# Cross-attention block: the order of the first row maxima, and batch 1 prepared before the first scores

## The chip, the cores and the metric

One core of one Trainium2 chip. The metric is the device time of one execution in microseconds (us), the median of three runs.

## The reference, cut to what matters

```python
B, S, D, H = 4, 512, 256, 16          # DK = 16 features per head; the context has 1024 keys
x = x + xattn(layernorm(x), ctx, ctx, mask)
x = x + ffn_block(layernorm(x))        # 4-token attention, then top-2 of 8 experts

def xattn(q, k, v, mask):
    query, key_, value = rope(heads(q @ w_q.T)), rope(heads(k @ w_k.T)), heads(v @ w_v.T)
    scores = einsum('bhqd,bhkd->bhqk', query, key_) / sqrt(DK)
    scores = where(mask == 0, -10000.0, scores)
    return merge(softmax(scores) @ value) @ w_o.T
```

The change lies in the cross-attention alone; the second block follows it and is the same in both kernels.

## The kernel before

**What is computed per batch.** For each of four batches `b` the kernel normalizes and turns the queries' input (jobs `xn`, `xT`), projects queries, keys and values (`q`, `k`, `v`; `c` is the split of a half of the context, 512 keys, into a high and a low float32r part), rotates queries and keys (`rope`, part 2 for queries, parts 0 and 1 for the two halves of the keys) and stores the rotated pieces to `q_pieces` and `k_pieces` in HBM. From there they are loaded again, regrouped by head, into `qst` and `kst`, three buffers each, one for every unit of eight heads.

**Maxima, then scores.** The softmax subtracts a row maximum that is found beforehand. A quad is four heads of one batch; there are 16. For each quad, 16 jobs `max` (two pairs of heads `hp`, four tiles of queries `qt`, two halves of the keys `kh`) each make two score products on TensorE into one of two buffers `wide`, and VectorE reduces each buffer (L749). Then `nm` and `mxt` turn the maxima into rows, ScalarE copies them to `mxp` (L603), and two DMAs put them into `qst` (L382). Only then can the quad's scores be made: 8 groups to a quad, 128 groups in all. A group is four scores (L942), four exponentials on ScalarE (L609) and, one group later, four products with the values (L957).

**Who does what, in which order.** Each engine runs its instructions in a written order. `attention_order` gives it: the list `before` is the opening, up to the first scores, and the list `timed` puts each job at a time counted in groups. All engines follow that one order, each for the jobs that it has a part in. A projection comes in pieces: the projections of `before` are mostly whole (512 columns), those in `timed` halves of 256 columns, six matmuls each. In the opening, batch 0 is prepared whole, and the keys of batch 1 (`k`, 1, 0 before the maxima of quad 0, `k`, 1, 1 after them). `xn` and `xT` of batch 1 stand in groups 0 and 2, its queries in groups 4 to 7, its values in groups 13 to 20. `xn` is four VectorE instructions (L701) from SBUF to SBUF.

**The queue of SP.** Stores and loads stand in one order of their own on SP, each with its waits, so an issue waits for all those ahead of it. In the opening it is:

```python
        store_turned(0, 2)                 # queries of batch 0
        store_turned(0, 1)                 # keys of batch 0, half 1
        load_keep(1, 0)
        load_queries(0, slice(0, 2))
        load_keys(0, slice(0, 2), (1,))
        load_queries(0, slice(2, PAIRS))
        store_turned(0, 0)
        load_keys(0, slice(0, 2), (0,))
        load_keys(0, slice(2, PAIRS))
        load_context(1, 1)
```

then unit 1, `load_keep(1, 1)`, `load_max_rows(0)` and the stores of batch 1's keys. The rotation of batch 1 and later is GpSimd's (L449 to L463), which also splits these context halves (L497, L466).

Of the kernel before, what the change touches and what calls it, by code (L numbers as in the profile page):

```python
# [36 lines left out]
LEAD = 3  # L37


def final(order, *begin):  # L40

    return next(j for j in reversed(order) if j[:len(begin)] == begin)


def attention_order():


    def maxes(quad):
        return [("max", quad, hp, qt, kh) for hp in range(2) for qt in range(QT) for kh in range(2)] + [("nm", quad), ("mxt", quad)]
# [4 lines left out]
    before += [("rate", 1), ("c", 1, 0), ("k", 1, 0, 0), ("k", 1, 0, 1), ("rope", 1, 0), ("c", 1, 1)] + maxes(0)  # L54
    before += [*maxes(1)[:2], ("k", 1, 1, 0), *maxes(1)[2:AHEAD], ("k", 1, 1, 1), ("rope", 1, 1)]

    timed = []
    for b in range(B):
        g, t = 32 * b, b + 1
        if t < B:  # L60
            timed += [(max(g - 3.5, 0), ("xn", t)), (g + (0.5 if b else 2.5), ("xT", t))]
            timed += [(g + x, ("q", t, n // 2, n % 2)) for n, x in enumerate((3, 4, 6, 7) if b else (4, 5, 6, 7))] + [(g + 7.5, ("rope", t, 2))]
            timed += [(g + 13.2 + n, ("v", t, n // 4, n // 2 % 2, n % 2)) for n in range(8)]
        if t + 1 < B:
            timed += [(g + 16.5, ("c", t + 1, 0)), (g + 20.5, ("c", t + 1, 1))]
            timed += [(g + 21.2 + n, ("k", t + 1, n // 4, n // 2 % 2, n % 2)) for n in range(8)] + [(g + 24.5, ("rope", t + 1, 0)), (g + 28.5, ("rope", t + 1, 1))]
        if b > 0:
            timed += [(g + 2.2, ("oT", b - 1))] + [(g + x, ("oP", b - 1, n // 2, n % 2)) for n, x in enumerate((8, 10, 11, 12))]
# [38 lines left out]
def cross_attention(nc, ctx, io, xt, wide, narrow, values, ident, mv1, rates, split_dram, list_dram):  # L107
# [3 lines left out]
    def sb(name, shape, dt=F32):  # L111
        return ctx.enter_context(nc.sbuf_tensor(name, shape, dt))
# [14 lines left out]
    rstd = sb("rstd", [P, NT])  # L127
    xT_hi = sb("xT_hi", [P, KC, SQ], F32R)
# [24 lines left out]
    aT_lo = sb("aT_lo", [P, KC, SQ], F32R)  # L153
    mask_i, mask_s = attn[0:B * KT, 0, 0:P].bitcast(I32), attn[0:B * KT, 1, 0:P]
# [8 lines left out]
    c_in, first_in, quad_in = sem("c_in"), sem("first_in"), sem("quad_in")  # L163
# [8 lines left out]
    var_set, std_set = sem("var_set"), sem("std_set")  # L172
# [12 lines left out]
    def on_act(j):  # L185
        return j[0] in ("w", "xT", "v", "mxt", "oT", "oT0", "oT1", "root0") or (j[0] in ("q", "k") and not turned_by_dve(j))
# [4 lines left out]
    def on_dve(j):  # L191
        return j[0] in ("xn", "xT", "max", "nm", "out", "oT", "oT0", "oT1", "oP", "oP1", "moments", "tile0", "again0", "rates0") or j in (("c", 0, 0), ("c", 0, 1)) or j in BY_DVE or (j[0] in ("q", "k") and turned_by_dve(j)) or (j[0] == "w" and not lo_by_pool(j))
# [108 lines left out]
    c_blocks = [(j[1], j[2]) for j in order if j[0] == "c" and j[1:] != (0, 0)]  # L301
# [9 lines left out]
    def _(sp):  # L311
# [32 lines left out]
        def landed(u, heads):  # L344
            return quad_in if u == 0 and heads.start == 0 else stack_in[u % 3]
# [123 lines left out]
    def _(pool):  # L469
# [20 lines left out]
        for j in order:  # L490
            if not on_pool(j):
                continue
            if j[0] == "c":
                b, g = j[1:]
                pool.wait_ge(c_in, 16 * (c_blocks.index((b, g)) + 1))
                pool.wait_ge(*by_pe(last_of("v", b - 1, g)))
                step(nc.gpsimd.tensor_copy(c_hi[g][:, :, :], craw[:, :, :]))  # L497
                settle()
                lower(nc.gpsimd, c_lo[j[2]], craw, c_hi[j[2]]).then_inc(pool_done, 1)
# [44 lines left out]
    def _(act):  # L544
# [15 lines left out]
        def job(j):  # L560
# [89 lines left out]
    def _(dve):  # L650
# [6 lines left out]
        def settle():  # L657

            dve.wait_ge(dve_step, steps[0])

        def statistics(i, batches):
# [13 lines left out]
            settle()  # L675

# [6 lines left out]
        for j in order:  # L683
# [12 lines left out]
            if kind == "xn":  # L696
                b = j[1]
                if b > 0:
                    dve.wait_ge(*by_pe(("xT", b - 1)))
                for t in range(QT):  # L700
                    last = nc.vector.tensor_scalar(xn[:, t, :], xt[:, QT * b + t, :], mv[:, QT * b + t, 0:1],  # L701
                                                   rstd[:, QT * b + t:QT * b + t + 1], ALU.subtract, ALU.mult)
# [107 lines left out]
    def _(pe):  # L810
# [60 lines left out]
        def job(j):  # L871
# [14 lines left out]
            if kind == "xT":  # L886
                pe.wait_ge(*by_dve(("xn", j[1])))
# [1028 lines left out]
```

## Time and profile before

| | us |
|---|---|
| median of 3 runs | 795.62 (795.46 to 797.01) |
| the profiled execution | 792.0 |
| its span in the trace | 790.2 |
| first matmul of the maxima | 61.14 |
| first matmul of the scores | 88.68 |
| copy of `outT` of the last quad | 509.7 |

TensorE is busy for 698.4 us (88%), VectorE 562.5 (71%), ScalarE 488.0 (62%), GpSimd 355.1 (45%). Times in the trace count from the span's start. `L621` is the copy of `outT` that ScalarE makes at the end of each quad, so the differences between its starts time eight groups each. "PEclk" is the clock that TensorE was granted: 1.00 is 2.4 GHz and 0.50 is 1.2 GHz.

### The profile page before, as it was taken

The numbers are of one execution on the slowest core, as the hardware profiler recorded it, in microseconds if no ns is written. First come the engines' busy times: TensorE is split into PE (matmuls) and PEld (weight loads), VectorE is DVE, ScalarE is ACT, GpSimd is POOL, SyncE is SP. The second block draws the span as 40 slices with busy tenths as digits, with TensorE's granted clock in tenths as the row PEclk, the third lists the DMA queues.
The fourth block names the chain that finished last, engine by engine and source line by source line (L and its number), as shares of the span: only waits on it lengthen the run. The fifth ranks groups of instructions, "written<-read, shape, count | busy, mean of one in ns | idle before, by whom it ended". The sixth has DMA issues, their size and how long they took to land. (4 is left out here: it accounts for less than half of the span.)

```text
span 790.2 us, 13501 instructions
## 1 busy us (share of the span) xinstructions
PE 698.4 (88%) x4402; PEld 428.4 (54%) x4402; DVE 562.5 (71%) x930; ACT 488.0 (62%) x968; POOL 355.1 (45%) x262
## 2 busy tenths in 40 slices
PE   3256689999999998999999999988978889999996
PEld 2252334444344443444433443476767779999995
DVE  4958778778788778788798984367997426555653
ACT  2010348777677776777778777856746047667673
POOL 4966425118604139345938880000045713544444
PEclk9775769999899999999999999999989799999999
DMA  9576246766667664326877870059736546623321
GB/s 256 187 235 183 104 150 190 229 160 204 213 207 243 174 187 160 115 83 197 292 250 244 274 265 6 1 156 409 249 67 179 223 109 143 117 31 40 39 28 20
DMA packets 59719, 130.73 MB, mean 165 GB/s; under 512 B 8868, under 2 KB 26308, under 8 KB 58196
## 3 DMA queue, kind: packets, MB, share of 16 engines
q1 hardware_dynamic: 33364, 72.86, 28.4%
q0 software_dynamic: 16848, 35.95, 17.8%
q10 hardware_dynamic: 9440, 21.06, 9.0%
q8 instruction: 38, 0.62, 0.3%
q14 instruction: 29, 0.24, 0.1%
HBM read 80.80 MB, written 69.39 MB: 190 GB/s over the span
## 5 line engine op out<-in xcount | busy, mean ns | idle before, releaser
L749 DVE TENSOR_REDUCE mx<-wide 128x2 f32<-128x1024 f32 x256 | 307.5, 1223 | 76.4 <-PE wide L903 74.9
L609 ACT ACTIVATE probs<-narrow 128x512 f32<-128x512 f32 x492 | 265.5, 599 | 87.7 <-PE narrow L942 86.6
L903 PE MATMUL wide<-kst,qst 49*128 49x512 f32 x512 | 181.1, 481 | 22.2 <-DVE mx L749 12.6
L942 PE MATMUL narrow<-qst,kst 51*128 51x512 f32 x492 | 188.8, 458 | 1.9 <-ACT probs L609 1.5
L942 PEld LDWEIGHTS narrow<-qst,kst 51*128 51x128 f32 x492 | 80.7, 189 | 135.8 <-issue 57.9
L957 PE MATMUL values<-probs,vaug 128*17 128x512 f32 x1024 | 139.0, 616 | 1.4 <-ACT probs L609 0.8
L1707 POOL DMA_INDIRECT out<-res,token x39 | 60.8, 1558 | 91.4 <-DMA out<-res,token 60.3
L903 PEld LDWEIGHTS wide<-kst,qst 49*128 49x128 f32 x512 | 74.7, 199 | 36.6 <-DVE mx L749 23.1
L454 POOL TENSOR_TENSOR turn_b<-turn_a,tab 128x1024 f32<-128x1024 f32 x10 | 24.1, 2410 | 69.8 <-ACT turn_a L603 69.2
L1239 POOL DMA_DIRECT2D out<-xt x4 | 5.5, 1376 | 108.5 <-DVE xt L1434 108.5
L1732 ACT ACTIVATE h_hi<-narrow 128x512 fp32r<-128x512 f32 x39 | 23.3, 598 | 41.3 <-PE narrow L1812 41.3
L1758 DVE TENSOR_TENSOR h_lo<-narrow,h_hi 128x512 fp32r<-128x512 f32 x39 | 27.0, 692 | 23.4 <-ACT h_hi L1732 23.4
L957 PEld LDWEIGHTS values<-probs,vaug 128*17 128x17 f32 x1024 | 17.1, 96 | 44.7 <-issue 30.0
L1246 POOL DMA_INDIRECT list_rows<-lists,rows_to x32 | 32.3, 1008 | 17.2 <-issue 8.5
L1754 DVE TENSOR_TENSOR y_lo<-y_full,y_hi 128x256 fp32r<-128x256 f32 x39 | 16.6, 426 | 28.9 <-ACT y_hi L1719 28.9
L449 POOL TENSOR_SCALAR keep<-keep 128x512 f32<-128x512 int32 x7 | 13.7, 1962 | 50.3 <-ACT turn_a L603 50.3
L1719 ACT ACTIVATE y_hi<-wide,lncol 128x128 fp32r<-128x128 f32 x78 | 36.3, 465 | 0.0
L1718 ACT ACTIVATE y_full<-wide,lncol 128x128 f32<-128x128 f32 x78 | 35.8, 459 | 0.1
L497 POOL CAST c_hi<-craw 128x1024 fp32r<-128x1024 f32 x6 | 6.2, 1037 | 60.7 <-PE narrow L817 57.9
L603 ACT ACTIVATE mxp<-narrow 8x512 f32<-8x512 f32 x16 | 9.2, 574 | 33.2 <-PE narrow L908 33.2
L603 ACT ACTIVATE vaug<-narrow 128x256 f32<-128x256 f32 (+1 forms) x28 | 11.7, 418 | 28.5 <-PE narrow L817 27.4
L817 PE MATMUL narrow<-wv_hi,c_hi 128*128 128x256 f32 x64 | 16.5, 343 | 14.3 <-POOL wv_lo L466 14.3
(287 smaller groups left out, 1370.1 us busy)
## 6 DMA issues: line engine op xcount, KB each, us to landing
list_rows<-in_w ACTq DMA_DIRECT2D x56, 342.0 KB, 4.7
kst<-k_pieces SPq DMA_DIRECT2D x14, 784.0 KB
k_pieces<-turn_a SPq DMA_DIRECT2D x16, 512.0 KB, 4.6
w_hi<-w_hi SPq DMA_DIRECT2D x16, 512.0 KB, 10.8
w_lo<-w_lo SPq DMA_DIRECT2D x16, 512.0 KB, 11.6
turn_a<-in_w POOLq DMA_DIRECT2D x11, 512.0 KB, 5.6
w_hi<-turn_b POOLq DMA_DIRECT2D x11, 512.0 KB, 3.0
w_lo<-turn_a POOLq DMA_DIRECT2D x11, 512.0 KB, 4.7
```

Source lines behind the costliest of these rows:

```text
L454: step(engine.tensor_tensor(z[:, :, :], a[:, :, :], cos, ALU.mult))
L609: nc.scalar.activation(probs[:, n % NP, :], score_bank(n), ACT.Exp, scale=DK ** -0.5).then_inc(exp_done, 1)
L749: last = nc.vector.tensor_reduce(mx[quad % 2][:, qt, :, hp, kh], slot[:, :, :], axis=AX.X, op=ALU.max)
L903: last = nc.tensor.matmul(slot[:, i, :], qst[u % 3][r:r + R_MAX, h, P * qt:P * qt + P], kst[u % 3][r:r + R_MAX, h, 512 * kh:512 * kh + 512 ...
L942: nc.tensor.matmul(score_bank(n), kst[u % 3][r:r + R_ALL, h, P * kt:P * kt + P], qst[u % 3][r:r + R_ALL, h, :], start=True, stop=True).the ...
L957: last = nc.tensor.matmul(values[32 * hq:32 * hq + DK + 1, :], vaug[b % 2][:, kt, h, :], probs[:, (4 * g + hq) % NP, :], start=kt == 0, st ...
L1246: pool.indirect_dma_start(list_dram, bass.IndirectOffsetOnAxis(rows_to[:, j, i, s:s + 1], 0), lists[j][:, i, s, :].bitcast(U32), None).the ...
L1707: pool.indirect_dma_start(out, bass.IndirectOffsetOnAxis(token[:, n:n + 1], 0), res[n % PIECES][:, :], None, bounds_check=TOKENS - 1, oob_ ...
L1718: nc.scalar.activation(yT[n % 2][:, k, :], y_banks[n % 2][:, k, :], ACT.Identity, **affine)
L1719: last = nc.scalar.activation(yT_hi[n % 2][:, k, :], y_banks[n % 2][:, k, :], ACT.Identity, **affine)
L1732: nc.scalar.activation(hT_hi[n % 2][:, :, :], h_banks[n % 2], ACT.Copy).then_inc(h_hi_set, 1)
L1758: nc.vector.tensor_tensor(hT_lo[n % 2][:, :, :], h_banks[n % 2], hT_hi[n % 2][:, :, :].bitcast(F32), ALU.subtract).then_inc(h_lo_set, 1)
```

## The change

1. The 16 maxima of quad 0 are made in another order: the eight on keys of half 1 first, then the eight on half 0. The first waits for the queries and half 1 alone (`quad_in`, 64); the ninth waits for half 0 (`half_in`, 32). SP issues the store and the load of half 0 ahead of the queries of pairs 2 and 3.
2. The second half of batch 1's context gets a buffer of its own (`next_raw`, which is `xn`'s memory), loaded at about 20 us, and leaves its place after unit 0's loads.
3. Batch 1's keys come as eight half pieces, one after each of the first eight maxima; its values, formerly in groups 13 to 20, as eight half pieces after the maxima 9 to 12, after `nm` and after the first two maxima of quad 1. `xT` of batch 1 stands after the eighth maximum.
4. `xn` of batches 1 to 3 goes to ScalarE, as one activation per tile with scale `rstd` and bias `shift` (one new small VectorE instruction), for batches 2 and 3 one tile to a group.
5. `PLAN` gives the places of all jobs of batches 2 and 3 in the groups, and SP's order in the loop is changed to fit. For batch 2: `c` in groups 3 and 12 (before 16 and 20), keys in 9 to 19 (before 21 to 28), `xn` in 18 to 21 (before 28), `xT` in 24 (before 32), queries in 26 to 30 (before 35 to 39), values in 36 to 44 (before 45 to 52). Batch 1's queries stand in groups 2 to 5.

```diff
+PLAN = [(18, (26, 27, 28, 30), (), (3, 12), (9, 10, 11, 14, 16, 17, 18, 19), ()),
+        (None, (), (4, 5, 6, 7, 9, 10, 11, 12), (7, 16), (18, 19, 20, 22, 23, 24, 25, 27), (13, 14, 15, 16)),
+        (-6, (3, 4, 6, 7), (13, 14, 15, 16, 17, 18, 19, 20), (), (), (8, 10, 11, 12)),
+        (None, (), (), (), (), (8, 10, 11, 12))]
...
-    before += [("rate", 1), ("c", 1, 0), ("k", 1, 0, 0), ("k", 1, 0, 1), ("rope", 1, 0), ("c", 1, 1)] + maxes(0)
-    before += [*maxes(1)[:2], ("k", 1, 1, 0), *maxes(1)[2:AHEAD], ("k", 1, 1, 1), ("rope", 1, 1)]
+    before += [("rate", 1), ("c", 1, 0), ("c", 1, 1)] + [("xn", 1, n) for n in range(QT)]
+    keys, vals = [[(kind, 1, n // 4, n // 2 % 2, n % 2) for n in range(8)] for kind in "kv"]
+    first = [("max", 0, hp, qt, kh) for kh in (1, 0) for hp in range(2) for qt in range(QT)]
+    for n, j in enumerate(first):
+        before += [j] + (keys + vals)[n:n + 1] * (n < 12) + [("rope", 1, 0)] * (n == 3) + [("rope", 1, 1)] * (n == 7) + [("xT", 1)] * (n == 7)
+    before += [("nm", 0), vals[4], vals[5], ("mxt", 0)] + maxes(1)[:2] + vals[6:] + maxes(1)[2:AHEAD]
...
+        sp.wait_ge(*by_pe(("xT", 0)))
+        sp.dma_start(next_raw, io["ctxT"][:, SK + 512:2 * SK].rearrange("(k p) t -> p k t", p=P)).then_inc(next_in, 16)
...
         load_keys(0, slice(0, 2), (1,))
-        load_queries(0, slice(2, PAIRS))
         store_turned(0, 0)
         load_keys(0, slice(0, 2), (0,))
+        load_queries(0, slice(2, PAIRS))
         load_keys(0, slice(2, PAIRS))
-        load_context(1, 1)
...
+            if t + 1 < B:
+                load_context(t + 1, 1)
             load_max_rows(4 * b + 2)
             if t < B:
                 load_queries(2 * t)
+            load_max_rows(4 * b + 3)
             if t + 1 < B:
-                load_context(t + 1, 1)
-            load_max_rows(4 * b + 3)
+                store_turned(t + 1, 0)
             if t < B:
                 load_queries(2 * t + 1)
                 load_keys(2 * t + 1)
                 load_max_rows(4 * b + 4)
             if t + 1 < B:
-                store_turned(t + 1, 0)
                 store_turned(t + 1, 1)
...
+            if kind == "xn":
+                b, t = j[1:]
+                if t == 0:
+                    act.wait_ge(*by_pe(("xT", b - 1)))
+                    if b == 1:
+                        act.wait_ge(*by_pool(("c", 1, 1)))
+                    act.wait_ge(shift_set, 1)
+                n = QT * b + t
+                nc.scalar.activation(xn[:, t, :], xt[:, n, :], ACT.Identity, scale=rstd[:, n:n + 1], bias=shift[:, n:n + 1]).then_inc(act_done, 1)
...
-                if (quad, hp, qt, kh) == (0, 0, 0, 0):
-                    pe.wait_ge(quad_in, 96)
+                if (quad, hp, qt) == (0, 0, 0):
+                    pe.wait_ge(*((quad_in, 64) if kh == 1 else (half_in, 32)))
```

## Rows read from the trace of the kernel before

**Rows 1.** Page, the span in 40 slices: granted TensorE clock in tenths.

```profile
PEclk9775769999899999999999999999989799999999
```

**Rows 2.** Windows; columns: PE, PEld, DVE, ACT, POOL busy, PEclk, DMA share, GB/s.

```profile
140.00:180.00 40.00, 40.00 (x272) 18.87 (x272) 31.04 (x33) 31.63 (x64) 6.86 (x4) 1.00 0.70 200
```

**Rows 3.** Timeline 40 to 62 us: start, duration, engine, line, operands, idle before.

```profile
43.96 0.66 SPq L371 DMA_DIRECT2D kst<-k_pieces  x2
...
45.73 1.04 POOL L497 CAST c_hi<-craw 128x1024 fp32r<-128x1024 f32 x1 [3.53 <-PE narrow L817]
45.76 0.42 SPq L339 DMA_DIRECT2D k_pieces<-turn_a  x1
...
46.85 2.39 POOL L466 TENSOR_TENSOR c_lo<-craw,c_hi 128x1024 fp32r<-128x1024 f32 x1
...
50.69 0.23 DVE L674 RECIPROCAL rstd<-std 128x12 f32<-128x12 f32 x1 [0.28 <-ACT std L565]
...
55.87 1.41 SPq L371 DMA_DIRECT2D kst<-k_pieces  x4
...
61.14 1.22 PE L903 MATMUL wide<-kst,qst 49*128 49x512 f32 x4 [8.76 <-DMA kst<-k_pieces]
```

**Rows 4.** Timeline 62 to 92 us: quad 0's maxima and the first scores.

```profile
62.05 18.19 DVE L749 TENSOR_REDUCE mx<-wide 128x2 f32<-128x1024 f32 x16 [11.13 <-PE wide L903]
...
82.07 0.59 ACT L603 ACTIVATE mxp<-narrow 8x512 f32<-8x512 f32 x1 [29.06 <-PE narrow L908]
82.69 1.45 SPq L382 DMA_DIRECT2D qst<-mxp  x2
...
88.68 0.50 PE L942 MATMUL narrow<-qst,kst 51*128 51x512 f32 x1
...
90.81 1.55 ACT L609 ACTIVATE probs<-narrow 128x512 f32<-128x512 f32 x3
```

**Rows 5.** Source L328, the load of `keep` issued at 59.5 us: landing.

```profile
DMA to landing us min/median/max: 23.8/23.8/23.8
```

**Rows 6.** Windows, while unit 1's keys are loaded.

```profile
74.00:78.00 4.00, 2.69 (x8) 0.86 (x6) 4.00 (x5) 0.00 (x0) 0.66 (x1) 0.50 0.44 180
```

**Rows 7.** Timeline 89 to 112 us: `xn`, `xT` of batch 1, a rotation on GpSimd.

```profile
89.47 1.94 POOL L449 TENSOR_SCALAR keep<-keep 128x512 f32<-128x512 int32 x1 [14.81 <-ACT turn_a L603]
...
91.50 2.40 POOL L451 TENSOR_TENSOR turn_a<-turn_a,keep 128x1024 f32<-128x1024 f32 x1
...
93.36 6.89 DVE L701 TENSOR_SCALAR xn<-xt,mv,rstd 128x256 f32<-128x256 f32 x4
...
102.55 2.35 POOL L463 TENSOR_TENSOR turn_b<-turn_b,turn_a 128x1024 fp32r<-128x1024 f32 x1
...
106.96 1.97 PE L890 MATMUL wide<-ident,xn 128*128 128x128 f32 x8 [0.89 <-DVE mx L749]
...
108.96 1.02 ACT L603 ACTIVATE xT_hi<-wide 128x1024 fp32r<-128x1024 f32 x1 [2.62 <-PE wide L890]
...
109.30 0.45 SPq L321 DMA_DIRECT2D craw<-in_ctxT  x1
...
110.09 1.22 DVE L727 TENSOR_TENSOR xT_lo<-wide,xT_hi 128x1024 fp32r<-128x1024 f32 x1 [2.05 <-PE wide L903]
```

**Rows 8.** Windows in the two stalls after `xn`.

```profile
96.00:98.00 2.00, 0.00 (x0) 0.00 (x0) 2.00 (x2) 0.00 (x0) 1.92 (x2) 0.81 0.00 0
196.00:200.00 4.00, 1.65 (x11) 0.75 (x8) 3.93 (x9) 1.73 (x4) 3.92 (x3) 0.95 0.19 73
```

**Rows 9.** Source L621 in successive windows: count, ns, first and last start.

```profile
L621 ACT ACTIVATE outT<-values x3: 598/600/606, 127.6 to 178.8; 128x512 f32<-128x512 f32 x3
...
L621 ACT ACTIVATE outT<-values x4: 597/598/599, 209.4 to 290.4; 128x512 f32<-128x512 f32 x4
...
L621 ACT ACTIVATE outT<-values x1: 599/599/599, 237.1 to 237.1; 128x512 f32<-128x512 f32 x1
...
L621 ACT ACTIVATE outT<-values x4: 597/597/599, 320.6 to 399.8; 128x512 f32<-128x512 f32 x4
...
L621 ACT ACTIVATE outT<-values x1: 597/597/597, 374.5 to 374.5; 128x512 f32<-128x512 f32 x1
...
L621 ACT ACTIVATE outT<-values x1: 600/600/600, 422.0 to 422.0; 128x512 f32<-128x512 f32 x1
```

**Rows 10.** DMA view, issues: KB each, median us to landing.

```profile
craw<-in_ctxT SPq DMA_DIRECT2D x7, 512.0 KB, 6.6
```

**Rows 11.** Groups on ScalarE after 600 us: count, busy and mean ns.

```profile
L1719 ACT ACTIVATE y_hi<-wide,lncol 128x128 fp32r<-128x128 f32 x78 | 36.3, 465 | 0.0
...
L1734 ACT ACT_TABLE_LOAD x1 | 1.3, 1283 | 19.3 <-PEq L1882 19.3
```

More of the change, by code:

```diff
@@ L59, in attention_order @@
         g, t = 32 * b, b + 1
[L60 to L66, printed above, removed]
+        x, q, v, c, k, o = PLAN[b]
+        if b == 0:
+            timed += [(n + 2.2, ("q", 1, n // 2, n % 2)) for n in range(4)] + [(5.5, ("rope", 1, 2))]
+        if x is not None:
+            r = 2 if b == 0 else t
+            timed += [(g + x + n, ("xn", r, n)) for n in range(QT)] + [(g + x + 6.2, ("xT", r))]
+            timed += [(g + at + 0.2, ("q", r, n // 2, n % 2)) for n, at in enumerate(q)] + [(g + q[-1] + 0.5, ("rope", r, 2))]
+        timed += [(g + at + 0.2, ("v", t, n // 4, n // 2 % 2, n % 2)) for n, at in enumerate(v)]
+        if k:
+            timed += [(g + at + 0.5, ("c", t + 1, n)) for n, at in enumerate(c)]
+            timed += [(g + at + 0.2, ("k", t + 1, n // 4, n // 2 % 2, n % 2)) for n, at in enumerate(k)] + [(g + k[4 * n + 3] + 0.5, ("rope", t + 1, n)) for n in range(2)]
         if b > 0:
-            timed += [(g + 2.2, ("oT", b - 1))] + [(g + x, ("oP", b - 1, n // 2, n % 2)) for n, x in enumerate((8, 10, 11, 12))]
+            timed += [(g + 2.2, ("oT", b - 1))] + [(g + at + 0.2, ("oP", b - 1, n // 2, n % 2)) for n, at in enumerate(o)]
     for quad in range(QUADS - 1):
@@ L95, in attention_order @@
     for b in range(1, B):
-        assert index[("xT", b - 1)] < index[("xn", b)] and index[final(order, "q", b - 1)] < index[("xT", b)]
+        assert index[("xT", b - 1)] < index[("xn", b, 0)] and index[final(order, "q", b - 1)] < index[("xT", b)]
         assert all(index[final(order, "v", b - 1, g)] < index[("c", b, g)] for g in range(2))
@@ L127, in cross_attention @@
     rstd = sb("rstd", [P, NT])
+    shift = sb("shift", [P, NT])
     xT_hi = sb("xT_hi", [P, KC, SQ], F32R)
@@ L185, in on_act @@
     def on_act(j):
-        return j[0] in ("w", "xT", "v", "mxt", "oT", "oT0", "oT1", "root0") or (j[0] in ("q", "k") and not turned_by_dve(j))
+        return j[0] in ("w", "xT", "v", "mxt", "oT", "oT0", "oT1", "root0") or j[0] == "xn" and j[1] > 0 or (j[0] in ("q", "k") and not turned_by_dve(j))
     def lo_by_pool(j):
@@ L191, in on_dve @@
     def on_dve(j):
-        return j[0] in ("xn", "xT", "max", "nm", "out", "oT", "oT0", "oT1", "oP", "oP1", "moments", "tile0", "again0", "rates0") or j in (("c", 0, 0), ("c", 0, 1)) or j in BY_DVE or (j[0] in ("q", "k") and turned_by_dve(j)) or (j[0] == "w" and not lo_by_pool(j))
+        return j[0] in ("xT", "max", "nm", "out", "oT", "oT0", "oT1", "oP", "oP1", "moments", "tile0", "again0", "rates0") or j in (("xn", 0),) or j in (("c", 0, 0), ("c", 0, 1)) or j in BY_DVE or (j[0] in ("q", "k") and turned_by_dve(j)) or (j[0] == "w" and not lo_by_pool(j))
     def on_pool(j):
@@ L299, in set_before @@
         return in_sets[in_sets.index(j) - 2] if j in in_sets[2:] else None
-    c_blocks = [(j[1], j[2]) for j in order if j[0] == "c" and j[1:] != (0, 0)]
+    c_blocks = [(j[1], j[2]) for j in order if j[0] == "c" and j[1:] not in ((0, 0), (1, 1))]
     k_blocks = [j for j in blocks if j[2] < 2]
@@ L342, in stored, with landed @@
             sp.wait_ge(*sets_stored(("rope", b, part)))
-        def landed(u, heads):
-            return quad_in if u == 0 and heads.start == 0 else stack_in[u % 3]
+        def landed(u, heads, parts=(0, 1)):
+            if u == 0 and heads.start == 0:
+                return half_in if parts == (0,) else quad_in
+            return stack_in[u % 3]
         def freed(u):
@@ L494, in _ @@
                 b, g = j[1:]
[L495 removed]
+                if (b, g) == (1, 1):
+                    pool.wait_ge(next_in, 16)
+                else:
+                    pool.wait_ge(c_in, 16 * (c_blocks.index((b, g)) + 1))
+                raw = next_raw if (b, g) == (1, 1) else craw[:, :, :]
                 pool.wait_ge(*by_pe(last_of("v", b - 1, g)))
[L497 removed]
+                step(nc.gpsimd.tensor_copy(c_hi[g][:, :, :], raw))
                 settle()
[L499 removed]
+                nc.gpsimd.tensor_tensor(c_lo[g][:, :, :], raw, c_hi[g][:, :, :].bitcast(F32), ALU.subtract).then_inc(pool_done, 1)
             elif j[0] == "w":
@@ L675, in statistics @@
             settle()
+            if i > 0:
+                nc.vector.scalar_tensor_tensor(out=shift[:, tiles], in0=mv[:, tiles, 0], scalar=-1.0, in1=rstd[:, tiles], op0=ALU.mult, op1=ALU.mult).then_inc(shift_set, 1)
         def masks():
@@ L751, in _ @@
                 quad = j[1]
-                dve.wait_ge(*by_dve(("max", quad, 1, QT - 1, 1)))
+                dve.wait_ge(*by_dve(last_of("max", quad)))
                 step(nc.vector.tensor_reduce(nm[:, :, :, :], mx[quad % 2][:, :, :, :, :], axis=AX.X, op=ALU.max, negate=True))
```

16 lines of the change are left out of this document (7 added, 9 removed).

## The prediction

> **What bounds the kernel now.** I read the page's slices first, then the windows, the timeline of the opening, the waits in it, and at last the ends of the quads. From about 110 us to 500 us TensorE's clock is nearly always full; the digits below it stand at the start, near 200 and near 310 us [rows 1]. In an undisturbed stretch of the groups TensorE is busy all 40 us of 40, VectorE and ScalarE 31 to 32 [rows 2]: there only TensorE's work counts, and work of other engines costs only when TensorE has to wait for it.
>
> Before the groups it is otherwise. The first maxima wait for keys: SP issues the last of their loads at 55.87, after a store that it issued from 45.76, and TensorE starts at 61.14 after 8.8 us idle. The load of half 1 had been issued at 43.96, and VectorE was free from 50.92 [rows 3]. The 16 maxima then take 18.19 us, 1.14 each, set by VectorE. `mxp` is ready at 82.66, its DMAs are issued from 82.69, the first score starts at 88.68 (TensorE has 1.2 GHz and the keys of batch 1 in between) and the first exponential at 90.81, after a table load [rows 4]. Meanwhile SP's queue drains slowly: the load of `keep`, issued at 59.5, lands 23.8 us later, at 83.3 [rows 5], while the DMA engines move only 180 GB/s at a share of 0.44, as if about 7 of the 16 worked [rows 6]. The key loads cover 49 partitions each; what stands behind them on those engines waits.
>
> Inside the groups there are three stalls. `xn` of batch 1 takes 6.89 us on VectorE beside GpSimd's rotation [rows 7]; TensorE is idle throughout 96 to 98 and loses its clock, and the same comes after `xn` of batch 2, with 1.65 us busy of 4 [rows 8]. The quads' ends price them [rows 9]. Groups 88 to 95 hold no projection and take 422.0 - 399.8 = 22.2 us. Groups 80 to 87 hold five half pieces and take 25.3, so a half piece costs 3.1 / 5 = 0.62. Groups 24 to 31, with five pieces and `xn`, take 209.4 - 178.8 = 30.6, where 22.2 + 3.1 = 25.3 would do: 5.3 lost. Groups 56 to 63, alike, take 30.2: 4.9 lost. Groups 32 to 39 with four pieces, `xT` and `oT` take 27.7, so `xT` and `oT` cost 3.0 together. The first eight groups take 127.6 - 88.7 = 38.9.
>
> **The change, part by part. The opening.** The first maximum needs the queries and half 1 alone. Half 0's load was used 61.14 - 55.87 = 5.3 us after its issue, so half 1, issued at 43.96, is there by about 50; VectorE is free at 51.2 (50.92 and `shift`, about as long as `rstd`). First maximum reduced from about 52 instead of 62.05: -10. The second context half costs no time: loaded at 20 us while TensorE's data is in hand, split on GpSimd right after the first (cast 1.04 and difference 2.39, so done near 52.8) [rows 3]; ScalarE's four `xn` follow to about 54.5, under 0.5 each (a copy four times as large took 1.02 [rows 7]). They block the key pieces' copies until then, but three pieces fit the ring, and the fourth comes near 55.5: no stall. Eight maxima with a key piece each: TensorE has 0.62 for the piece and up to 0.5 for the pair, VectorE 1.14; I take 1.2 a step, 9.6, to 61.6. If the clock were 1.2 GHz, a step would cost 1.24 for the piece and 0.8 for the pair (four matmuls took 1.22 [rows 3]), 2.0, which I keep for the upper end. `xT`: transposes 1.97 at half clock, copy 1.02, difference 1.22 [rows 7]; one transposing step overlaps the last maximum, so 2.8 net, to 64.4. Eight more maxima, four with a value piece: 4 x 1.2 + 4 x 1.14 = 9.4, to 73.8. From the last maximum's end (80.24) to `mxp`'s (82.66) it was 2.4 [rows 4]: 76.2. SP then issues the rows until 77.7.
>
> Here stands the choice. If the rows land at once, about 1.5 us after, scores start near 79; the last pieces and four maxima of quad 1 fill TensorE until then. If the rows queue behind unit 1's keys as `keep` did, they wait until the queue drains. That was at 83.3. In the new order half 0's store is issued 0.4 us sooner and without 384 KB of queries in front, and 512 KB of context are gone behind it; at the rates of [rows 6] that is some 2 us: 81.2. I take the queue, since a DMA issued on it did wait 23.8 us [rows 5], and scores from 81.7: **-7.0**. The ends are 79 and 85. The Trainium skill (DMA: Bandwidth & Descriptors, "Why a DMA increments its semaphore by 16 and not by 1") says that a transfer issued from SP is split over the largest number of engines up to 16 that divides the outermost dimension, the lowest-numbered of them: 7 for 49 partitions, 2 for the row pairs. By that rule the rows are on two of the seven loaded engines and queue; without it the sum would be 2.7 lower. The trace agrees so far as the share of 0.44 goes [rows 6].
>
> **Groups 0 to 7.** They lose `xn`, `xT`, the stretch at half clock and the table load, which now falls into the wait for the rows. What stays is 22.2 + 4 x 0.62 = 24.7, and 2.3 for the lag from a first score to a quad's end and two groups with three maxima (3.4 of VectorE against about 2.8): 27.0 for 38.9, **-11.9**.
>
> **Groups 8 to 63** took 320.6 - 127.6 = 193.0 [rows 9]. In `PLAN` they hold 32 pieces (4, 4, 4, 4, 7, 6, 3 by quad) where there were 40: 7 x 22.2 + 32 x 0.62 + 3.0 = 178.2. (The same for before: 183.2, and 10 of stalls is what [rows 9] showed.) Eight of `xn` now cut into ScalarE's exponentials, 0.4 each; ScalarE has 8.4 of 40 us free [rows 2], 0.6 a group, so most of it fits, and I add 1.5 for what delays an exponential.
>
> Then the moved jobs' due times. `keep` for rotation (1, 1) lands near 81.2 now as well. A rotation takes 89.47 to 104.90 = 15.4; its store, two `keep` loads and the context's issue took from 104.9 to 109.3 = 4.4 [rows 7]; the context lands 6.6 after that [rows 10] and its split is 3.5: 111.1, against the key pieces due at the end of group 9, near 112. Batch 1's query rotation behind it on GpSimd takes 15.4 less its first two instructions (4.3) = 11.1, to 122.2. Behind its store on SP now stand context (2, 1) and the maxima's rows of quad 2, which land at 122.2 + 2.4 for the issues + 6.6 = 131.2, and the split at 134.7; due are the rows at group 16, near 131, and the pieces at its end, near 134. So two items are just in time or late by a microsecond or two: +2. Together 178.2 + 1.5 + 2 = 181.7: **-11.3**. From group 64 on the order is the same, and the second block too: 0. Its weights are split by GpSimd after the last rotation, in the same group as before.
>
> **Sum.** -7.0 - 11.9 - 11.3 = -30.2. Against the profiled execution's 792.0 that is 761.8; the median is 3.6 above the profiled one, so 765.4, said as 765.
>
> **Rivals.** *Slow clock and late chain.* TensorE had 1.2 GHz while it made maxima alone [rows 6], and it may keep it in the opening, since VectorE paces it again. Twelve steps at 2.0 instead of 1.2 are +9.6, from 76.2 to 85.8 for `mxp`, scores near 89.5: +7.8; or group 16 waits 5 us and loses 3 more of clock. 773 to 781. For it: [rows 1, 8]. Against: a piece's 0.62 doubles TensorE's work in those steps.
>
> *Rows not held up.* The rows land at once: 762.5, inside my range.
>
> *Chain decides (slower).* In SP's queue, store of batch 1's queries, context and rows of quad 2 hang on GpSimd, which hangs on `keep`. Every microsecond past group 16's start is TensorE's, and once it passes the 30 saved elsewhere, near 163 us for the rows, the kernel is slower: two rotations more than I count, and 800 or above. Nothing in the rows asks for two.
>
> *The function table.* If `Identity` had to reload ScalarE's table between exponentials, each `xn` would cost two loads of 1.28: eight are 20.5, and 4.9 more in the opening hidden, so 786, and near no change with the clock lost too. Against: 78 activations of that kind stand beside the gelu with one load before them all [rows 11].
>
> *The early start gives nothing.* The rows queue to 85: opening -3.7 instead of -7.0: 769.
>
> **Chances.** Forecast with its near cases (rows at 79 to 85): 0.70, alone 758 to 772. Slow clock or late chain: 0.18. Table: 0.04. Chain decides, or something like it: 0.04. No effect for another reason: 0.02. Better than the sum (stalls cost more than counted): 0.02. The range 755 to 781 takes in the first two. What a measurement can tell from no change is 0.2%, 1.6 us. Faster 0.93, same 0.02, slower 0.05.
>
> **What would show it.** First `max` matmul near 51 to 52; first score at 80 to 83, its wait ended by the DMA of `mxp`; end of quad 0 near 109; 24 to 26 us for each of the quads 1 to 3, no window of idle TensorE near 200 or 310. Wrong would be: half 1 landing after 55; clock 0.50 through the maxima; a wait at group 9 or 16 for a split or for rows of over 3 us; table loads among the exponentials.

## The result: 1.1% faster, and outside the range

| | before | changed |
|---|---|---|
| median, same chip (us) | 796.2 (795.46 to 797.01, 4 runs) | 787.93 (783.22 to 791.12, 4 runs) |
| profiled execution, its span | 792.0, 790.2 | 785.13, 783.3 |
| first score | 88.68 | 86.14 |
| end of quad 0, end of quad 15 | 127.6, 509.7 | 115.6, 499.3 |

The ratio is 0.9886, with a 95% interval of 0.9838 to 0.9934: 8 us of gain where 30 were forecast, and a time above the upper end of the range.

The ends of the quads again are the starts of the copy of `outT`, now L653, in successive windows; they answer to [rows 9].

```profile
L653 ACT ACTIVATE outT<-values x3: 598/598/598, 115.6 to 166.3; 128x512 f32<-128x512 f32 x3
...
L653 ACT ACTIVATE outT<-values x1: 599/599/599, 270.5 to 270.5; 128x512 f32<-128x512 f32 x1
...
L653 ACT ACTIVATE outT<-values x1: 597/597/597, 306.3 to 306.3; 128x512 f32<-128x512 f32 x1
...
L653 ACT ACTIVATE outT<-values x2: 598/598/599, 336.0 to 362.2; 128x512 f32<-128x512 f32 x2
...
L653 ACT ACTIVATE outT<-values x6: 597/598/653, 387.8 to 499.3; 128x512 f32<-128x512 f32 x6
```

Six quads, groups 8 to 55, take 270.5 - 115.6 = 154.9. Then groups 56 to 63 take 306.3 - 270.5 = 35.8 where they took 30.2, and the next eight 29.7. The windows show both places: the old stall near 200 us is gone, a new one stands at 293 to 303 us, and with it comes the slow clock. They answer to [rows 8].

```profile
196.00:200.00 4.00, 4.00 (x27) 2.08 (x28) 3.60 (x5) 2.85 (x6) 3.07 (x2) 1.00 0.89 290
292.00:296.00 4.00, 1.64 (x12) 0.36 (x12) 2.61 (x3) 1.94 (x4) 3.77 (x5) 1.00 0.47 178
296.00:300.00 4.00, 0.00 (x0) 0.00 (x0) 0.00 (x0) 0.00 (x0) 2.21 (x1) 0.50 0.55 210
300.00:304.00 4.00, 0.78 (x4) 0.50 (x4) 0.00 (x0) 0.00 (x0) 0.00 (x0) 0.50 0.95 344
```

What TensorE waits for there is in the waits of 272 to 306 us (us in total, times, longest):

```profile
PE narrow L972 <- DMA qst<-mxp: 9.6, 1, 9.6
```

Those are the maxima's rows of quad 8. SP's queue in the timeline of that stretch shows what was issued just ahead of them:

```profile
281.58 0.38 SPq L353 DMA_DIRECT2D k_pieces<-turn_a  x1
...
283.37 2.76 SPq L374 DMA_DIRECT2D qst<-q_pieces  x2
286.24 0.95 SPq L387 DMA_DIRECT2D kst<-k_pieces  x2
288.82 1.29 SPq L398 DMA_DIRECT2D qst<-mxp  x2
```

In the kernel before, the same rows had 27 us between the loads of unit 5 and themselves, and the stores came behind them (its timeline, 280 to 316 us):

```profile
283.55 0.80 SPq L358 DMA_DIRECT2D qst<-q_pieces  x2
284.46 0.61 SPq L371 DMA_DIRECT2D kst<-k_pieces  x2
311.44 1.28 SPq L382 DMA_DIRECT2D qst<-mxp  x2
312.76 0.40 SPq L339 DMA_DIRECT2D k_pieces<-turn_a  x1
```

The change put the store of batch 3's first keys, ready at 281, ahead of unit 5's loads, so these were issued just ahead of the rows; 8 KB then landed at 303.2, 14.4 us after their issue. While TensorE stood still the DMA engines moved 178 to 210 GB/s at a share of 0.47 to 0.55, the picture of [rows 6].

The opening, in the timeline from 48 us, which answers to [rows 3, 4]:

```profile
48.64 0.50 PE L933 MATMUL wide<-kst,qst 49*128 49x512 f32 x2 [1.74 <-DMA kst<-k_pieces]
...
49.08 2.04 DVE L704 TENSOR_SCALAR varc<-mv 128x12 f32<-128x12 f32 x1
...
51.75 3.48 DVE L779 TENSOR_REDUCE mx<-wide 128x2 f32<-128x1024 f32 x3
...
58.46 1.23 DVE L779 TENSOR_REDUCE mx<-wide 128x2 f32<-128x1024 f32 x1 [1.07 <-PE wide L933]
...
79.39 2.36 POOL L469 TENSOR_TENSOR turn_a<-turn_a,keep 128x1024 f32<-128x1024 f32 x1
79.67 0.19 DVE L783 TENSOR_REDUCE nm<-mx 128x16 f32<-128x32 f32 x1
79.89 1.88 DVE L787 CAST mh<-nm 128x16 fp32r<-128x16 f32 x1
...
83.38 1.45 SPq L398 DMA_DIRECT2D qst<-mxp  x2
...
85.45 1.28 ACT L658 ACT_TABLE_LOAD   x1
...
86.14 0.50 PE L972 MATMUL narrow<-qst,kst 51*128 51x512 f32 x1
```

The first maximum starts even sooner than forecast. Then VectorE, which should pace these steps, waits 1.07 us in each for TensorE: a step takes 2.3 us, with the clock at 0.50 from 50.2 to 67.3 us. The page shows the clock over the whole span, beside [rows 1]; the dip near 300 us is the stall above.

```profile
PEclk9767799999999995999999999999998889999999
```

### The profile page after: what moved, and what is told of

Read it like the earlier page. It is cut to its first block and busy times, and to the rows that moved or that the text cites. A ratio compares the mean times of both kernels' runs of the same rounds, so it can differ in the third digit from the quotient of the medians.

```text
span 783.3 us, 13563 instructions
## 1 busy us (share of the span) xinstructions
PE 701.2 (90%) x4426; PEld 433.2 (55%) x4426; DVE 559.5 (71%) x919; ACT 494.7 (63%) x984; POOL 354.7 (45%) x262
## 3 DMA queue, kind: packets, MB, share of 16 engines
q1 hardware_dynamic: 33364, 72.86, 27.7%
## 5 line engine op out<-in xcount | busy, mean ns | idle before, releaser
L933 PE MATMUL wide<-kst,qst 49*128 49x512 f32 x512 | 174.3, 467 | 7.3 <-DVE mx L779 3.9
L972 PEld LDWEIGHTS narrow<-qst,kst 51*128 51x128 f32 x492 | 80.1, 188 | 144.3 <-ACT probs L641 53.5
L987 PE MATMUL values<-probs,vaug 128*17 128x512 f32 x1024 | 137.3, 608 | 1.4 <-ACT probs L641 0.8
L933 PEld LDWEIGHTS wide<-kst,qst 49*128 49x128 f32 x512 | 71.7, 191 | 19.4 <-DVE mx L779 12.5
L472 POOL TENSOR_TENSOR turn_b<-turn_a,tab 128x1024 f32<-128x1024 f32 x10 | 24.1, 2412 | 58.6 <-ACT turn_a L635 58.1
L1748 ACT ACTIVATE y_full<-wide,lncol 128x128 f32<-128x128 f32 x78 | 35.8, 460 | 2.2 <-PE wide L1819 2.2
L847 PE MATMUL narrow<-wv_hi,c_hi 128*128 128x256 f32 x64 | 16.6, 345 | 14.4 <-POOL wv_lo L484 14.4
L1833 PE MATMUL wide<-w_hi,y_hi 128*128 x78 | 28.6, 448 | 0.0
```

Source lines behind the costliest of these rows:

```text
L933: last = nc.tensor.matmul(slot[:, i, :], qst[u % 3][r:r + R_MAX, h, P * qt:P * qt + P], kst[u % 3][r:r + R_MAX, h, 512 * kh:512 * kh + 512 ...
L972: nc.tensor.matmul(score_bank(n), kst[u % 3][r:r + R_ALL, h, P * kt:P * kt + P], qst[u % 3][r:r + R_ALL, h, :], start=True, stop=True).the ...
L987: last = nc.tensor.matmul(values[32 * hq:32 * hq + DK + 1, :], vaug[b % 2][:, kt, h, :], probs[:, (4 * g + hq) % NP, :], start=kt == 0, st ...
L1748: nc.scalar.activation(yT[n % 2][:, k, :], y_banks[n % 2][:, k, :], ACT.Identity, **affine)
L1833: last = nc.tensor.matmul(up_banks[n % 2], a[n % 2][:, k, :], w[:, bass.ds(e, 1), k, :].rearrange("p e n -> p (e n)"), start=(i, k) == (0, ...
```

## The experiments

The first four kernels ran beside the kernel before on one chip, the next four on a second, the last three on a third. On the second and third, what follows the end of quad 15 takes 293 to 296 us and not 283 to 285, so medians are compared as ratios to the kernel before on the same chip. The expectations give times for the first chip: a ratio of 0.9715 would be 773.5 us there, 0.9633 would be 767.0. In the table `A` is the end of quad 0 and `B` the time from there to the end of quad 15, both in the profiled execution.

| kernel | A | B | ratio, 95% interval |
|---|---|---|---|
| before | 127.6 | 382.1 | 1 |
| changed | 115.6 | 383.7 | 0.9886, 0.9838 to 0.9934 |
| `a_loads_first` | 119.1 | 384.3 | 0.9866, 0.9835 to 0.9898 |
| `b_rows_first` | 118.4 | 382.4 | 0.9842, 0.9783 to 0.9901 |
| `c_xn_scalar` | 117.4 | 376.7 | 0.981, 0.9783 to 0.9837 |
| `d_opening_alone` | 116.6 | 378.4 | 0.9858, 0.983 to 0.9886 |
| `e_loads_first_once` | 117.3 | 370.5 | 0.9715, 0.9669 to 0.9761 |
| `f_rows_by_scalar` | 116.4 | 404.4 | 1.017, 1.0105 to 1.0236 |
| `g_filled_gap` | 110.5 | 371.3 | 0.9633, 0.9591 to 0.9676 |
| `h_keys_ahead` | 114.6 | 371.5 | 0.9733, 0.9666 to 0.98 |
| `i_changed_again` | 112.6 | 387.4 | 0.9847, 0.9796 to 0.9897 |
| `j_old_groups` | 114.5 | 372.3 | 0.9633, 0.9602 to 0.9663 |
| `k_clock_held` | 113.5 | 370.3 | 0.9678, 0.9651 to 0.9706 |

`B` holds a wait that differs between two executions of the same program. Groups 96 to 103 take 23.9 us in the kernel before and 24.3 in the changed one, but 28.3 when the changed one ran again (`i_changed_again`) and 28.4 in `d_opening_alone`. In `i_changed_again` VectorE's cast to `mh` falls beside an instruction of GpSimd there and ends with it:

```profile
421.38 2.36 POOL L556 TENSOR_TENSOR turn_a<-turn_a,turn_b 128x1024 fp32r<-128x1024 f32 x1
...
421.48 2.29 DVE L787 CAST mh<-nm 128x16 fp32r<-128x16 f32 x1
```

TensorE waits 1.5 us for it, and the clock is at 0.50 from 424.9 to 431.7 us. (`a_loads_first` has a cast of 2.27 us at that place but keeps its clock: 26.2.) So the windows of single quads say more than `B` where a difference is under 5 us.

**Unit loads ahead of the store, in every batch** (`a_loads_first`).

```diff
             load_max_rows(4 * b + 3)
-            if t + 1 < B:
-                store_turned(t + 1, 0)
             if t < B:
                 load_queries(2 * t + 1)
                 load_keys(2 * t + 1)
+            if t + 1 < B:
+                store_turned(t + 1, 0)
+            if t < B:
                 load_max_rows(4 * b + 4)
```

> The changed kernel with one move in SP's loop: unit 5's (and 3's) queries and keys are issued before the store of the next batch's keys, not after it. Theory 1: in the changed kernel the maxima's rows of quad 8 land late because they are issued right behind the keys of unit 5, which had waited behind that store; TensorE idles 9.6 us at group 64 and then works at half clock. Then the quad of groups 56 to 63 falls from 35.8 us to 24 to 26, the next from 29.7 to 27 to 28, and the kernel is 11 to 14 us faster than the changed one: 774 to 777. Rival: the late rows are caused by ScalarE's normalizations in groups 58 to 61 delaying the maxima; then the quad stays above 32 us and the time above 783.

The quads' ends put groups 56 to 63 at 25.2 us, so that stall was the order of SP's queue. But groups 24 to 31 now take 37.8. Now it is the store of batch 2's keys that stands behind unit 3's, in the timeline of SP's queue, the waits of 176 to 196 us and a window:

```profile
165.44 0.84 SPq L387 DMA_DIRECT2D kst<-k_pieces  x2
166.33 0.57 SPq L353 DMA_DIRECT2D k_pieces<-turn_a  x1
```

```profile
ACT turn_a L636 <- DMA k_pieces<-turn_a: 10.4, 1, 10.4
...
PE narrow L973 <- ACT turn_a L636: 9.2, 1, 9.2
```

```profile
184.00:188.00 4.00, 0.00 (x0) 0.00 (x0) 0.00 (x0) 0.00 (x0) 0.00 (x0) 0.60 0.25 98
```

ScalarE can't free the piece's buffer before the store has landed, its exponentials wait behind it, and TensorE waits for them: whatever stands right behind a unit's key load pays.

**Rows ahead of the unit loads** (`b_rows_first`): `load_max_rows(4 * b + 4)` moved ahead of `load_queries(2 * t + 1)`, the store first.

> The changed kernel, the store left where the change put it, but the rows of quads 4 and 8 issued before the loads of queries and keys of units 3 and 5. Theory 1: only the place behind the keys matters, so the gain is the same as with the loads first, 11 to 14 us against the changed kernel, 774 to 777, unless the keys themselves then come late for quads 6 and 10. Rival (the store itself, 1.5 MB, holds the rows up): gain under 5 us, 783 or more.

Groups 56 to 63 take 25.2 again, but groups 32 to 39 take 32.3. The rows of quad 5 wait behind the unit load and all that has heaped up behind it, in the waits of 212 to 230 us:

```profile
PE narrow L972 <- DMA qst<-mxp: 4.3, 1, 4.3
```

**Unit 5 alone** (`e_loads_first_once`): as `a_loads_first`, but only where `b == 1`.

> The changed kernel with unit 5's loads ahead of the store of batch 3's keys, the first pass of the loop (unit 3) left as the change has it. Theory 1 (whatever SP issues behind a pair of key loads lands late, be it rows or a store): the quads of groups 24 to 31 and 32 to 39 as in the changed kernel (25.7 and 26.3), those of 56 to 63 and 64 to 71 at 25.2 and 27.7 as with both moved; no wait of over 4 us left in the groups; 774 to 777. Rival (a stall merely moves to the next place): 783 or more.

No stall is left: groups 56 to 63 take 25.2 and the next eight 27.7, `B` falls by 13.2 to 370.5. The timeline has the loads at 266 us and 23 us between them and the rows:

```profile
265.96 0.88 SPq L374 DMA_DIRECT2D qst<-q_pieces  x2
266.95 0.61 SPq L387 DMA_DIRECT2D kst<-k_pieces  x2
...
283.21 0.38 SPq L353 DMA_DIRECT2D k_pieces<-turn_a  x1
...
290.46 1.28 SPq L398 DMA_DIRECT2D qst<-mxp  x2
```

**The rows from ScalarE's queue** (`f_rows_by_scalar`). Does the wait lie in SP's order of issue, or behind the bytes?

```diff
             nc.scalar.activation(dst, src, ACT.Copy).then_inc(act_done, 1)
+            if kind == "mxt":
+                rows_by_scalar(act, j[1])
```

> The changed kernel, but the DMAs of the maxima's rows are issued by ScalarE right after the copy to mxp, so they stand in ScalarE's queue; SP's order else as changed. If the rows wait because they stand in one queue behind the keys, the wait at group 64 goes: that quad near 25, 774 to 779, with some 0.5 to 1 us for each quad's two issues on ScalarE. If they wait because the engines are full whatever the queue, the quad stays above 32 us and the time above 783.

The rows still wait: groups 56 to 63 take 34.4 us, above the 32 of the second branch, and the kernel is 1.7% slower than before. In the waits of 290 to 330 us:

```profile
PE narrow L978 <- DMA qst<-mxp: 7.6, 1, 7.6
```

There is a new wait as well. SP no longer waits for a quad's rows before it issues a unit's loads, so unit 3's loads go out at 156.7 to 160.2 us, ahead of the rows of quad 3, and these, on a queue of their own, still land 10.6 us after their issue. In the timeline:

```profile
162.20 1.41 ACTq L583 DMA_DIRECT2D qst<-mxp  x2
...
172.85 0.79 PE L978 MATMUL narrow<-qst,kst 51*128 51x512 f32 x1 [4.69 <-DMA qst<-mxp]
```

So the rows wait behind the bytes of the key load, not behind SP's instructions. The Trainium skill (DMA: Bandwidth & Descriptors, "Why a DMA increments its semaphore by 16 and not by 1") has transfers issued from either queue use the lowest-numbered engines, so that a second queue brings no other engines; this run agrees. `B` is 404.4 us, 20.7 more than in the changed kernel. The new wait and ScalarE's 1.4 us for each quad's two issues are in it; how much each costs is not settled.

**xn on ScalarE alone** (`c_xn_scalar`): the kernel before, with part 4 of the change and nothing else.

```diff
-            timed += [(max(g - 3.5, 0), ("xn", t)), (g + (0.5 if b else 2.5), ("xT", t))]
+            timed += [(g - 3.5 + n if b else 0.5 * n, ("xn", t, n)) for n in range(QT)] + [(g + (0.5 if b else 2.5), ("xT", t))]
```

> The kernel before with one part of the change: the normalization of batches 1 to 3 goes to ScalarE, one tile to a group (batch 1: two in group 0 and two in group 1), all else as before. By my step (stalls of 5.3 and 4.9 us after it in groups 24 to 31 and 56 to 63, and some 6 to 9 in groups 0 to 7 with the lost clock, less 1.5 for ScalarE): 778 to 783, 13 to 18 us faster. Rival (the stalls come from the transposes of xT or the maxima that follow, which stay): 790 or more.

781.1 against 796.9: this part alone gives 15.8 us, twice what the whole change gives. Groups 24 to 31 take 26.6 for 30.6, groups 56 to 63 26.6 for 30.2, and quad 0 ends 10.2 sooner. The window near 200 us holds no idle TensorE:

```profile
196.00:200.00 4.00, 3.98 (x25) 1.75 (x24) 3.06 (x3) 3.43 (x7) 3.85 (x4) 1.00 0.56 172
```

**The opening alone** (`d_opening_alone`): the changed kernel's opening, and the groups, SP's loop and `xn` of batches 2 and 3 as before.

> The changed opening with the order of batches 2 and 3 and SP's loop as before, normalization of batches 2 and 3 on VectorE as before. First score near 86 as in the changed kernel, quad 0 ends near 116, eight value pieces fewer in the groups (-4.6), the stalls at groups 28 and 60 and their clock as before. By the sum of the two traces: 12 at quad 0's end and 4.6 for the pieces, so 778 to 781. Rival (the early start is given back by late loads in quads 1 to 3, which the new order of batch 2 was needed for): 785 or more.

0.9858, 11 us. In the trace `A` falls by 11.0, where the forecast had 18.9 for the opening and groups 0 to 7; the first score starts at 87.8 us, behind 2.3 us steps again. The eight value pieces that leave the groups are worth the 5.0 us forecast: groups 8 to 23 take 46.2 for 51.2. `B` falls by 3.7 alone because groups 96 to 103 take 4.5 more, by the wait told above.

The two `xn` stalls tell something more. `xn` is on VectorE, and TensorE waits 2.3 us for the quad's maxima behind it, as in the kernel before [rows 8], but here the clock stays at 1.00:

```profile
180.00:184.00 4.00, 1.71 (x12) 0.77 (x8) 3.93 (x9) 1.85 (x4) 3.92 (x3) 1.00 0.19 73
```

Groups 24 to 31 take 28.0 us, for 30.6 in the kernel before (whose clock is at 0.50 from 199.6 to 206.5) and 26.6 in `c_xn_scalar`. So of the 4.0 us of that stall about 1.4 are the wait and 2.6 the slow clock behind it, which this kernel's profile doesn't have.

**The clock in the opening** (`g_filled_gap`): `e_loads_first_once`, and 14 small matmuls, whose result nothing uses, ahead of the first maximum.

```diff
+                if j == ("max", 0, 0, 0, 1):
+                    for i in range(14):
+                        nc.tensor.matmul(slot[:, 0, 0:P], ident[:, :], ident[:, :], start=True, stop=True)
```

> As e_loads_first_once, with 14 unused 128-column matmuls on TensorE before the first maximum, where it waits for the keys. Theory 2 (the first eight steps take 2.3 us instead of 1.2 because TensorE is at half clock, and the clock falls for the idle time before the first maximum): clock 1.00 from 48 to 60, steps of 1.2 to 1.4, first score 6 to 8 us sooner, 768 to 771. Rival (the clock falls all the same, since maxima of 49 rows and VectorE's pace leave TensorE too idle): first score within 2 us of the changed kernel's, 774 to 777.

778.36 against 785.48 for `e_loads_first_once` on the same chip: 7.1 us. The filler closes TensorE's idle time ahead of the first maximum; then the clock is 1.00 from 48 to 72 us, and VectorE's eight reductions stand in one row without a wait. In its timeline:

```profile
48.08 3.29 PE L933 MATMUL wide<-ident 128*128 128x128 f32 x28
...
53.11 9.73 DVE L783 TENSOR_REDUCE mx<-wide 128x2 f32<-128x1024 f32 x8
...
75.22 0.17 DVE L791 CAST mh<-nm 128x16 fp32r<-128x16 f32 x1
```

**Four key pieces ahead of the first maximum** (`h_keys_ahead`), real work in the filler's place.

> As e_loads_first_once, but the four key pieces of half 0 of batch 1 stand before the first maximum, where TensorE waits anyway, those of half 1 between maxima 1 to 4, the values after the next eight. Theory 2: eight pieces at half clock in the way of the maxima become four, and dense work before them may hold the clock: first score 3 to 8 us sooner, 768 to 774. Rival (the place of the pieces is not what costs): within 2 us of e_loads_first_once.

784.96, no better than `e_loads_first_once`: the gap is filled, but four pieces delay the first maximum to 53.5 us, and the clock is slow at 75 to 99 us instead.

**The changed kernel again, on a third chip** (`i_changed_again`).

> The changed kernel itself, beside the other two on one chip, so that its own differences to them can be read without a change of chip. All theories: 0.985 to 0.99 of the kernel before; quad 7 (groups 56 to 63) 35 to 36 us and the next 29 to 30, since the rows of quad 8 stand behind unit 5's loads; clock at 0.50 from 50 to 67 us in the maxima with key pieces.

`B` has the stall (302.9 to 331.8 is 28.9 us for groups 64 to 71, the eight before them 35.9). The opening is the surprise. This execution of the very same program kept its clock:

```profile
52.60 9.71 DVE L779 TENSOR_REDUCE mx<-wide 128x2 f32<-128x1024 f32 x8
...
76.87 1.45 SPq L398 DMA_DIRECT2D qst<-mxp  x2
...
82.17 0.50 PE L972 MATMUL narrow<-qst,kst 51*128 51x512 f32 x1 [2.32 <-DMA qst<-mxp]
```

The window of 56 to 60 us is at 1.00 here,

```profile
56.00:60.00 4.00, 4.00 (x27) 2.87 (x26) 3.82 (x5) 1.15 (x3) 2.80 (x2) 1.00 0.82 209
```

and at 0.50 in the changed kernel's first profile, where TensorE gets 18 matmuls done instead of 27:

```profile
56.00:60.00 4.00, 4.00 (x18) 3.07 (x16) 2.45 (x2) 0.38 (x1) 1.80 (x1) 0.50 0.96 213
```

In both, TensorE was idle about 1.7 us for the keys just before the maxima. So the clock behind that gap differs from execution to execution. Of the six profiled executions in which TensorE was idle there for 1.3 to 2.2 us, five fell to 0.50 within 2 us of the first maximum, and this one did not. `f_rows_by_scalar`, idle for 0.4 us, kept 1.00, and so did the four kernels with the gap filled.

The spread of the times isn't this clock alone: it is 8 and 11 us for the changed kernel, 3.9 for `e_loads_first_once`, 2.8 for `g_filled_gap`, and the execution shown here took 796.95, 8 us above the fastest of its six, though its opening kept the clock.

**Before's groups, with the opening and xn** (`j_old_groups`): `g_filled_gap`'s opening, `xn` on ScalarE, but batches 2 and 3 in the groups of the kernel before and SP's old loop.

> The changed kernel's opening with the gap ahead of the first maximum filled by 14 small matmuls (they write nothing that is used), but batches 2 and 3 in the groups in which they stand in the kernel before, with SP's old order in the loop, and their xn on ScalarE, one tile to a group. Theory: of the changed kernel's last part (PLAN) nothing was worth time, only the three stalls that xn on ScalarE takes away and the opening were; then quads 1 to 14 take the same sum as in the version with the unit 5 loads moved (366 to 372 us from the end of quad 0 to that of quad 15), all quads 24 to 28.5, and the time is within 3 us of that version with the gap filled (0.963 to 0.967 of before where that one was 0.963). Rival: PLAN levels the pieces over the groups (28 at most to a quad would overload groups 24 to 31, where VectorE and ScalarE carry 8 pieces and xn at once), so the old order leaves waits of 1 to 2 us in each of the three heavy quads: 375 us or more, ratio 0.97 or above.

0.9633, the same as `g_filled_gap`, and `B` is 372.3 against 371.3. Its opening ran at 0.50 from 67.9 to 78.1 and from 84.9 to 98.6 us, so `A` is 4 us later. Within what the intervals leave, 3 us, `PLAN` brought nothing, and the order of SP's queue that came with it cost 13 us.

**Filler between the maxima too** (`k_clock_held`).

```diff
-                if j == ("max", 0, 0, 0, 1):
-                    for i in range(14):
+                fill = 14 * (j == ("max", 0, 0, 0, 1)) or 5 * (quad == 0 and hp == 1 and kh == 0) or 5 * (quad == 1 and hp == 0 and kh == 0)
+                for i in range(fill):
```

> The version with the gap filled and unit 5's loads moved, plus 5 small matmuls (128 columns, unused) ahead of each of the last four maxima of quad 0 and of the first four of quad 1. Theory: what is left of the slow clock in the opening (72.9 to 79.7 and 86.6 to 90 us) comes from TensorE being idle between maxima; with these steps filled the clock stays 1.00 from 48 us on, the value pieces after nm take 1.3 us instead of 2.7, the maxima's rows come 1 to 1.5 us sooner, first score near 80 instead of 81.5, quad 0's end near 109: ratio 0.002 to 0.003 below that of the version with one gap filled. Rival: the rows' landing, not TensorE, sets the first score (3.4 us from mxp to the score), and the filler delays maxima by its own length (8 times 0.27): no gain, first score 81 to 82.5.

In this edit the filler stands ahead of the last four maxima of quad 0 and of the first, third, fifth and seventh of quad 1, not of its first four. The clock is 1.00 from 44 to 494 us, and the time is no better: 0.9678. The filler writes to the buffer that the maximum needs, so it starts only when VectorE has released it, and a step grows from 1.14 to 1.74 us. First score 83.9, quad 0's end 113.5, 3.0 later than `g_filled_gap`.

## Why the prediction was wrong, by its own steps

Against the forecast of 479.5 for the end of quad 15 (509.7 - 30.2) the profiled execution has 499.3. The 19.8 us:

| step | forecast | measured | off by |
|---|---|---|---|
| first score | 81.7 | 86.1 | +4.4 |
| groups 0 to 7 | 27.0 | 29.5 | +2.5 |
| groups 8 to 55 | 154.1 + 3.5 | 154.9 | -2.7 |
| groups 56 to 63 | 24.1 | 35.8 | +11.7 |
| groups 64 to 71 | as before, 27.7 | 29.7 | +2.0 |
| groups 72 to 127 | as before, 161.4 | 163.3 | +1.9 |

(154.1 is 6 x 22.2 + 29 x 0.62 + 3.0, 24.1 is 22.2 + 3 x 0.62.) The second block adds 3.5, 284.0 for 280.5. The four kernels of the first chip had 283 to 285 too, whatever had been changed ahead of it, `c_xn_scalar` with nothing of the change but `xn` among them; and before's profiled execution was 4 us under its median. So I do not put it down to the change, though no run isolates it.

**The step that failed: groups 56 to 63.** The part "the moved jobs' due times" followed context (2, 1) and the rows of quad 2 down SP's queue, and then stopped. Of `store_turned(3, 0)`, moved ahead of `load_queries(5)`, nothing was said, though the mechanism that makes it dear was in the text, used for the opening: 8 KB of rows wait behind a unit's key load. The rows of quad 8 paid for it with 11.7 + 2.0 us, and `e_loads_first_once` gave back 12.6 in these two quads. "From group 64 on 0" was wrong by the clock that this stall left behind.

**The opening: off by the clock, and right at a full clock in part by luck.** With a full clock (`i_changed_again`) the steps take 9.71 for the eight where 9.6 was forecast, the rows are issued at 76.87 (76.2), wait for their DMA, and the first score starts at 82.2 (81.7): the choice "I take the queue" holds there. The load of `keep`, issued just ahead of the rows, landed at 81.8 in that execution, where the forecast had 81.2 for the queue; but it landed at 77.2 in the changed kernel's own profile and at 78.4 in `g_filled_gap`, whose first score starts at 80.9. So the agreement at 81.7 is in part luck. In the changed kernel's own profile the half clock put the rows' issue at 83.38, when the queue had drained; they landed 2.8 us after it. The rival "slow clock" was sized at 2.0 a step, measured 2.3; its condition, that VectorE paces and TensorE waits, was wrong: TensorE was busy all 4 us of 4 from 56 us on. A small VectorE instruction beside GpSimd added 1.7 us that were in no step: the cast to `mh` took 1.88, where it takes 0.17 with GpSimd idle (`g_filled_gap`). The cast ends at 81.77, and GpSimd's instruction beside it at 79.39 + 2.36 = 81.75; the reduction `nm`, which started inside the same GpSimd instruction, took its 0.19. Of the changed kernel's sixteen casts to `mh` eight overlap an instruction of GpSimd, and all eight end 0.03 to 0.04 us after it. `varc` took 2.04 in the same way, but the first reduction still started at 51.75, where about 52 was forecast. In `i_changed_again` `varc` started 0.05 us ahead of GpSimd's instruction and took 0.17; the next one, `shift`, then took 1.73. The Trainium skill (SBUF — State Buffer, "SBUF: two separate sides") has some VectorE instructions share a port pair with GpSimd as an exclusive lock, held for a whole instruction; the end of these casts agrees.

**Groups 0 to 7** took 29.5 for 27.0. The forecast had them lose "the stretch at half clock", and they did not: the clock was at 0.50 for 6.8 us behind the first scores (87.8 to 94.6). `d_opening_alone` had 3.4 us of it and took 28.8, `e_loads_first_once` 13.7 us and took 32.5. `k_clock_held` had a full clock and yet took 29.6, but ten of its filler matmuls lie in these groups, 2.8 us busy and 1.5 us of waiting ahead of them. Windows of the changed kernel and of `k_clock_held`, and the filler's group in the latter:

```profile
86.10:115.60 29.50, 28.62 (x168) 12.26 (x166) 25.58 (x24) 21.21 (x41) 16.22 (x11) 0.88 0.56 194
...
83.90:113.50 29.60, 28.02 (x188) 13.35 (x186) 24.96 (x24) 20.44 (x41) 18.37 (x11) 1.00 0.48 171
...
L933 PE MATMUL wide<-ident 128*128 128x128 f32 x20 | 2.8, 285 | 1.5 <-DVE mx L783 1.5
```

So the clock is the likely cause of most of the 2.5 us. No run has a full clock there without filler, so its share is not shown.

**Right:** the two `xn` stalls, if too large (forecast 5.3 and 4.9, `c_xn_scalar` gave back 4.0 and 3.6, more than half of it slow clock), `Identity` without further table loads, the 0.62 of a half piece, the rows and splits in time at groups 9 and 16 (the 3.5 us allowed for them and for ScalarE were not needed, though each `xn` took 0.60 us on ScalarE and not 0.4). By themselves `xn` brings 1.9% and the opening 1.4%, with batch 1's `xn` in both. Without the new wait the change brings 2.9% (`e_loads_first_once`), so the wait took back 1.7%, more than half. The forecast of 765 is 0.961 of the median of before. `g_filled_gap` has 0.9633, with the wait gone and with filler, which the forecast did not have, against the slow clock.

## What to carry to other kernels

When a store or a load moves in a queue, list every small transfer that comes behind it until the next long one, and check each against its due time, in every batch: a fault found in one pass of the loop (`a_loads_first`) may sit in another for the opposite order. A small transfer issued right behind a large one can take that one's time: 8 KB of rows landed 14.4 us after their issue here behind a unit's key load, and 10.6 us after it from another queue. And try the parts of a large change one by one: here one of five parts gave twice the whole.

## What was not expected of the hardware

The same program, with the same 1.7 us of idle TensorE at the same place, ran the next 17 us once at 1.2 GHz and once at 2.4 GHz, a difference of 6.5 us in the issue of the rows (83.38 against 76.87). In the slow stretch TensorE was busy 4.00 us of 4 from 56 us on, and the clock stayed at 0.50 until 67.3. 3.3 us of filler removed it in the profile taken, and in the two other kernels that had the same filler (`j_old_groups`, `k_clock_held`).

A cast of 16 elements a partition, 0.17 us with GpSimd idle, took up to 2.29 us beside GpSimd, as long as what was left of GpSimd's instruction. Inside the groups that went with up to 4.5 us more for a quad, where the clock fell behind the wait.
